# Chunk rows requested two steps sooner, and two heads' scores joined in one tile of two banks, in a gated cross-attention and feed-forward kernel

## What is computed

```python
def _layernorm(x, eps=1e-5): return (x - mean(x)) / sqrt(var(x) + eps)
def reference(x, ctx, mask, g_xattn, g_ffn, ...):      # x: 2 x 2048 x 512, ctx: 2 x 128 x 512
    # cross attention, 16 heads of 32, keys and values from ctx (128 rows of each batch)
    xn = layer_norm(_layernorm(x), g_x, b_x);  kvn = layer_norm(ctx, g_kv, b_kv)
    q = xn @ w_q;  k, v = split(kvn @ w_kv)
    attn = softmax(where(mask == 0, -1e9, q k^T * 32**-0.5));  out = attn v
    x = x + tanh(g_xattn) * (out @ w_proj + b_proj)
    # feed-forward, 512 -> 2048 -> 512, weights dequantised from integers and scales
    h = layer_norm(_layernorm(x), ln_gamma, ln_beta)
    z = silu(h @ w1 + fc1_bias) @ w2 + fc2_bias
    return x + tanh(g_ffn) * (x' + 0.5 * z)            # x' is the layer-normed input of the block
```

## Time and profile before

| | us |
|---|---|
| median of 3 runs (lowest, highest) | 1244.69 (1244.65, 1246.11) |
| profiled execution, its own time | 1246.29 |
| span of the profiled execution | 1244.7 |
| PE busy in the span | 1112.7 (89%) |
| DVE, ACT, POOL busy | 631.7, 388.1, 338.4 |
| attention stage, to the first feed-forward product | about 0 to 515 |

### The profile page before, as it was taken

One profiled execution on the slowest core, in us unless ns is written; L12 is line 12 of the kernel. 1 busy time (PEld: TensorE's weight loads), 2 busy tenths in 40 slices (PEclk: granted clock), 3 DMA queues, 4 the chain that ended last, 5 costly groups with the idle time before them and its releaser, 6 DMA issues.

```text
span 1244.7 us, 15876 instructions
## 1 busy us (share of the span) xinstructions
PE 1112.7 (89%) x5433; PEld 851.2 (68%) x5433; DVE 631.7 (51%) x1039; ACT 388.1 (31%) x614; POOL 338.4 (27%) x344
## 2 busy tenths in 40 slices
PE   5668779796978895899999999999999999999998
PEld 3345456464645563688888888888888888888887
DVE  6755757576675763777533533433434335235222
ACT  3347445464645573234111112111112111111110
POOL 4433546454554653401210210210111012012000
PEclk9779899898989898999999999999999999999999
DMA  6434353534444344790100100100100100100000
GB/s 241 94 92 107 84 141 88 139 96 117 113 124 132 82 120 140 253 316 10 36 33 1 64 5 1 68 1 1 67 0 0 67 0 0 68 1 1 34 1 34
DMA packets 56570, 92.44 MB, mean 74 GB/s; under 512 B 12952, under 2 KB 14144, under 8 KB 56000
## 3 DMA queue, kind: packets, MB, share of 16 engines
q1 hardware_dynamic: 55752, 91.54, 25.0%
q10 hardware_dynamic: 760, 0.14, 0.1%
HBM read 47.34 MB, written 16.78 MB: 52 GB/s over the span
## 4 chain that ended last, share of the span: by engine, by line
PE 58%; DVE 0%; issue 0%; ACT 0%; DVEq 0%
PE ps_y L220 10%; PE ps_y L219 10%; PE ps_y L218 9%; PE ps_z L1209 9%; PE ps_z L1211 9%; PE ps_z L1210 9%; PE ps_h L1223 1%; DVE x L1292 0%; DVE w_lo L176 0%; DVE w_f L170 0%; ACT w_hi L161 0%; DVE y_hi L1269 0%; ACT y_f L1244 0%; DVEq L47 0%; DVE y_lo L1271 0%
## 5 line engine op out<-in xcount | busy, mean ns | idle before, releaser
L1269 DVE CAST y_hi<-y_f 128x512 fp32r<-128x512 f32 x128 | 62.6, 489 | 390.7 <-ACT y_f L1244 390.7
L1244 ACT ACTIVATE y_f<-ps_y,cols 128x512 f32<-128x512 f32 x128 | 88.1, 689 | 551.7 <-PE ps_y L220 551.7
L218 PE MATMUL ps_y<-xt_hi,w_hi 128*128 128x512 f32 x512 | 202.5, 396 | 1.9 <-PEq L255 1.9
L220 PE MATMUL ps_y<-xt_hi,w_lo 128*128 128x512 f32 x512 | 204.1, 399 | 0.0
L1209 PE MATMUL ps_z<-w_hi,y_hi 128*128 128x512 f32 x512 | 202.6, 396 | 1.4 <-DVE w_lo L176 1.4
L219 PE MATMUL ps_y<-xt_lo,w_hi 128*128 128x512 f32 x512 | 203.5, 397 | 0.0
L1211 PE MATMUL ps_z<-w_hi,y_lo 128*128 128x512 f32 x512 | 200.1, 391 | 0.0
L1210 PE MATMUL ps_z<-w_lo,y_hi 128*128 128x512 f32 x512 | 199.9, 390 | 0.0
L218 PEld LDWEIGHTS ps_y<-xt_hi,w_hi 128*128 128x128 f32 x512 | 96.6, 189 | 25.2 <-issue 2.3
L219 PEld LDWEIGHTS ps_y<-xt_lo,w_hi 128*128 128x128 f32 x512 | 96.9, 189 | 22.9
L220 PEld LDWEIGHTS ps_y<-xt_hi,w_lo 128*128 128x128 f32 x512 | 96.5, 189 | 22.6
(11 more groups left out here) (161 smaller groups left out, 1593.1 us busy)
## 6 DMA issues: line engine op xcount, KB each, us to landing
q_pack<-q_hi SPq DMA_DIRECT2D x256, 64.0 KB, 2.0
x_in<-in_x SPq DMA_DIRECT2D x8, 1024.0 KB, 5.9
q_pack<-q_lo SPq DMA_DIRECT2D x128, 64.0 KB, 2.0
x_res<-in_x SPq DMA_DIRECT2D x32, 256.0 KB, 3.2
x_dram<-x_out SPq DMA_DIRECT2D x32, 256.0 KB, 3.3
q_raw<-in_L_ffn_fc_q SPq DMA_DIRECT2D x8, 1024.0 KB, 15.2
s_raw<-in_L_ffn_fc_scales SPq DMA_DIRECT2D x8, 1024.0 KB, 16.7
x_in<-x_dram SPq DMA_DIRECT2D x4, 1024.0 KB, 5.4
```

The costliest lines, as they stand in the source:

```text
L218: nc.tensor.matmul(out, s_hi, m_hi, start=(k == 0), stop=False)
L220: last = nc.tensor.matmul(out, s_lo, m_hi, start=False, stop=(k == n - 1))
L1244: nc.scalar.activation(y_f[f % 2][:, :], ps_y[f % 2][:, :], ACT.Silu, bias=b1_c[:, f:f + 1]).then_inc(y_f_ready, 1)
```

## The change

Two edits. First, `load_x` moves: chunk 0 is loaded at step -8 as before, and chunk c (1 to 8) at the head of SP's step 4c - 10 instead of 4c - 8. SP's steps are all written out now, none is in a hardware loop. Second, heads go in pairs: `ps_s` is one tensor of two banks, the scores of heads 0 and 1 fill it, then one `p_f` and one `p_hi` activation of 128x1024 empty it, and then heads 2 and 3 use it. DVE subtracts pair 0 in one instruction and POOL pair 1 in one. On PE the scores of heads 2 and 3 now stand behind both halves of the projection.

```diff
+        p_f = [sb(f"p_f{n}", [P, 2, CHUNK], F32) for n in range(2)]     (p_hi, p_lo alike)
-        ps_s = [psum("ps_s0"), psum("ps_s1")]
+        ps_s = scope.enter_context(nc.psum_tensor("ps_s", [P, 2, 512], F32))
...
-                if k % KB == 0:
-                    load_x(i, k // KB + 2)
+                if k == FIRST:
+                    load_x(i, 0)
+                if k % KB == 2:
+                    load_x(i, k // KB + 3)
...
-            every_step(sp, step, {-8: load_context, -7: load_weights, -3: pack_keys})
+            setup = {-8: load_context, -7: load_weights, -3: pack_keys}
+            for k in range(FIRST, LAST):
+                if k in setup:
+                    setup[k]()
+                step(0, k)
...
-                after(pe, p_hi_ready, HG * v + j - 1)
-                nc.tensor.matmul(ps_s[j % 2][:, :], k_pack[...], q_pack[...],
+                after(pe, p_hi_ready, 2 * v + j // 2)
+                nc.tensor.matmul(ps_s[:, j % 2, :], k_pack[...], q_pack[...],
                                  start=True, stop=True).then_inc(s_done, 1)
...
                 if real(i, k - 5, UNITS):
                     project(i, k - 5, first)
+                if real(i, k - 5, UNITS):
+                    project(i, k - 5, second)
                 if real(i, k, UNITS):
                     scores(i, k, 2)
                     scores(i, k, 3)
-                if real(i, k - 5, UNITS):
-                    project(i, k - 5, second)
...
-            def probabilities(i, k, j):
+            def probabilities(i, k, pair):
-                after(act, s_done, HG * v + j + 1)
-                after(act, p_lo_dve if j < HG // 2 else p_lo_pool, HG // 2 * (v - 1) + j % (HG // 2) + 1)
-                nc.scalar.activation(p_f[j][:, :], ps_s[j % 2][:, :], ACT.Exp, bias=fill_col[:, b:b + 1]).then_inc(p_f_ready, 1)
+                after(act, s_done, HG * v + 2 * pair + 2)
+                after(act, (p_lo_dve, p_lo_pool)[pair], v)
+                nc.scalar.activation(p_f[pair][:, :, :], ps_s[:, :, :], ACT.Exp, bias=fill_col[:, b:b + 1]).then_inc(p_f_ready, 1)
                 after(act, pv_done, v)
-                nc.scalar.activation(p_hi[j][:, :], ps_s[j % 2][:, :], ACT.Exp, bias=fill_col[:, b:b + 1]).then_inc(p_hi_ready, 1)
+                nc.scalar.activation(p_hi[pair][:, :, :], ps_s[:, :, :], ACT.Exp, bias=fill_col[:, b:b + 1]).then_inc(p_hi_ready, 1)
...
-                nc.vector.tensor_tensor(p_lo[j][:, :], p_f[j][:, :], p_hi[j][:, :], ALU.subtract).then_inc(p_lo_dve, 1)
+                nc.vector.tensor_tensor(p_lo[0][:, :, :], p_f[0][:, :, :], p_hi[0][:, :, :], ALU.subtract).then_inc(p_lo_dve, 1)
...
-                nc.gpsimd.tensor_tensor(p_lo[j][:, :], p_f[j][:, :], p_hi[j][:, :], ALU.subtract).then_inc(p_lo_pool, 1)
+                nc.gpsimd.tensor_tensor(p_lo[1][:, :, :], p_f[1][:, :, :], p_hi[1][:, :, :], ALU.subtract).then_inc(p_lo_pool, 1)
```

More of the change, by code:

```diff
@@ L287, in attention @@
             k_top, k_rest = (tmp(n, [P, KB, B * KEYS], F32R) for n in ("k_top", "k_rest"))
-        p_f = [sb(f"p_f{n}", [P, CHUNK], F32) for n in range(HG)]
-        p_hi = [sb(f"p_hi{n}", [P, CHUNK], F16) for n in range(HG)]
-        p_lo = [sb(f"p_lo{n}", [P, CHUNK], F16) for n in range(HG)]
+        p_f = [sb(f"p_f{n}", [P, 2, CHUNK], F32) for n in range(2)]
+        p_hi = [sb(f"p_hi{n}", [P, 2, CHUNK], F16) for n in range(2)]
+        p_lo = [sb(f"p_lo{n}", [P, 2, CHUNK], F16) for n in range(2)]
         inv_den, den_t = sb("inv_den", [P, CHUNK], F32), sb("den_t", [P, CHUNK // HEAD, HEAD], F32)
@@ L311, in attention @@
         ps_ctx, ps_cols = ps_max, ps_o
-        ps_k, ps_v = [ps_s[0], ps_s[1], ps_den, ps_max[0]], [ps_o, ps_den]
+        ps_k, ps_v = [ps_s[:, 0, :], ps_s[:, 1, :], ps_den, ps_max[0]], [ps_o, ps_den]
         (vec_loaded, ctx_loaded, mask_loaded, gate_loaded, wk_loaded, wv_loaded, wq_loaded, wp_loaded, bias_loaded, ident_ready,
@@ L514, in scores @@
                     after(pe, max_packed[k % 2], 16 * HG * (before_in_slot(i, k) + 1))
-                after(pe, p_hi_ready, HG * v + j - 1)
-                nc.tensor.matmul(ps_s[j % 2][:, :], k_pack[0:PACK, j, m, b * KEYS:(b + 1) * KEYS], q_pack[k % 2][0:PACK, j, :],
+                after(pe, p_hi_ready, 2 * v + j // 2)
+                nc.tensor.matmul(ps_s[:, j % 2, :], k_pack[0:PACK, j, m, b * KEYS:(b + 1) * KEYS], q_pack[k % 2][0:PACK, j, :],
                                  start=True, stop=True).then_inc(s_done, 1)
@@ L522, in weighted_values @@
                 v, b, m = PER * i + k, (k // KB) % 2, k % KB
-                after(pe, p_hi_ready, HG * (v + 1))
-                after(pe, p_lo_dve, HG // 2 * (v + 1))
-                after(pe, p_lo_pool, HG // 2 * (v + 1))
+                after(pe, p_hi_ready, 2 * (v + 1))
+                after(pe, p_lo_dve, v + 1)
+                after(pe, p_lo_pool, v + 1)
                 after(pe, o_f_ready, v)
@@ L530, in weighted_values @@
                         h = HG * m + j
-                        nc.tensor.matmul(ps_o[HEAD * j:HEAD * (j + 1), :], part[:, b, h * HEAD:(h + 1) * HEAD], probs[j][:, :],
+                        nc.tensor.matmul(ps_o[HEAD * j:HEAD * (j + 1), :], part[:, b, h * HEAD:(h + 1) * HEAD], probs[j // 2][:, j % 2, :],
                                          start=(n == 0), stop=(n == len(terms) - 1))
@@ L534, in weighted_values @@
                     for j in range(HG):
-                        last = nc.tensor.matmul(ps_den[HEAD * j:HEAD * (j + 1), :], ones16[:, :], probs[j][:, :],
+                        last = nc.tensor.matmul(ps_den[HEAD * j:HEAD * (j + 1), :], ones16[:, :], probs[j // 2][:, j % 2, :],
                                                 start=(n == 0), stop=(n == 1))
@@ L714, in step @@
                 if real(i, k, UNITS):
-                    for j in range(HG):
-                        probabilities(i, k, j)
+                    probabilities(i, k, 0)
+                    probabilities(i, k, 1)
                 if real(i, k - 1, UNITS):
@@ L810, in normalise, with probabilities_lo @@
                 nc.vector.tensor_tensor(o_f[k % 2][:, :], ps_o[:, :], inv_den[:, :], ALU.mult).then_inc(o_f_ready, 1)
[L812 removed]
+            def probabilities_lo(i, k):
                 v = PER * i + k
[L814 removed]
+                if isinstance(i, int) and v == 0:
                     dve.wait_ge(setup_over, 2)
[L816 to L818 removed]
+                after(dve, p_f_ready, 2 * v + 1)
+                after(dve, p_hi_ready, 2 * v + 1)
+                nc.vector.tensor_tensor(p_lo[0][:, :, :], p_f[0][:, :, :], p_hi[0][:, :, :], ALU.subtract).then_inc(p_lo_dve, 1)
             def add_residual(i, k):
@@ L983, in x_lo, with probabilities_lo @@
                                         ALU.subtract).then_inc(xt_lo_ready, 1)
-            def probabilities_lo(i, k, j):
+            def probabilities_lo(i, k):
                 v = PER * i + k
-                if isinstance(i, int) and v == 0 and j == 2:
+                if isinstance(i, int) and v == 0:
                     pool.wait_ge(setup_over, 2)
-                after(pool, p_f_ready, HG * v + j + 1)
-                after(pool, p_hi_ready, HG * v + j + 1)
-                nc.gpsimd.tensor_tensor(p_lo[j][:, :], p_f[j][:, :], p_hi[j][:, :], ALU.subtract).then_inc(p_lo_pool, 1)
+                after(pool, p_f_ready, 2 * v + 2)
+                after(pool, p_hi_ready, 2 * v + 2)
+                nc.gpsimd.tensor_tensor(p_lo[1][:, :, :], p_f[1][:, :, :], p_hi[1][:, :, :], ALU.subtract).then_inc(p_lo_pool, 1)
             def row_scales(i, c):
```

12 lines of the change are left out of this document (5 added, 7 removed).

## The result

The changed kernel takes 1191.87 us (median of 3 runs, 1190.06 to 1192.41) against 1244.69: a ratio of 0.957, 95% interval 0.955 to 0.959. The profiled execution has a span of 1190.5 us and a mean granted clock of 0.974. 1191.8 was predicted.

What follows compares the result with a forecast made beforehand. Load stalls bound attention before, SP's DMA issuing after. Terms -55.8 + 2.9 = -52.9 us take the profiled execution from 1246.3 to 1193.4, carried to the median as 1191.8 us; 8-of-10 range 1173 to 1208.

Steps and rivals of the forecast that it cites:

- The stalls: Seven chunk loads: the 8 us idle of DVE and PE goes, no PE wait for maxima over 1 us.
- The pairs: Ordinary attention step: two activations 2.2 us, pair 1 scores at 3.35, step 10.7 us, 0.5 less than now.
- SP after both: Attention runs at SP's pace, 11.69 us a step; 29 steps sum to 340.6 us, unit 31's maxima 55.8 us sooner.
- PE's wait in each step: In attention PE waits about 1 us for the copied maxima before the first pair of scores in each step.
- The end: Last attention unit: weighted values at 11.1 us after its scores, 2.9 us more with nothing to hide it.
- Rival A: Attention: SP is not the bound, chunks take the compute side's 44.3 us against SP's 47.4; 1173 us; chance 0.10.
- B: Attention: SP's step is 12.1 us, 12 us lost, 1204; up to 1220 with PE's clock lower; chance 0.16.
- C: Chunk load still late behind SP's own queue; only the pairs act, 0.5 us in 25 steps, 1232; chance 0.02.
- Rival D: Attention: waits in each step bring PE to 1.2 GHz, slower than before; fully low 1410 us; chance 0.02.
- a sign against itself: PE's clock falling in ordinary attention steps would show the prediction wrong; no size was given.

Runs made afterwards that it cites:

- Experiment 1: The kernel before with the earlier chunk load and SP's steps written out, but heads' scores apart as before: 1187.33 us, ratio 0.952.
- experiment 5: The changed kernel with the residual load and the store of a tile issued by ACT instead of SP: 1166.09 us, ratio 0.936.
- 6: The kernel before with early load and SP written out, heads apart, plus residual load and store issued by ACT instead of SP: 1181.45 us.
- experiment 3: The changed kernel with one more DMA of 512 bytes issued by SP in each of the steps 2 to 30: 1208.47 us.
- experiment 9: The changed kernel with the chunk's load behind the four copies of the maxima and ahead of the query copies in SP's step: 1191.20 us.
- Experiment 7: The changed kernel; in step 31 second-pair scores stand between the projection's halves, and SP issues weight loads behind the copied maxima: 1184.00 us.
- experiment 11: The changed kernel with residual load and store on ACT, step 31's second-pair scores between projection halves, weight loads behind copied maxima: 1168.09 us.

## Why the prediction was right, and where it was not

*The stalls.* Right: the wait for `x_in` is gone but for 0.3 us, PE's longest wait for maxima is 1.2 (1 was said). Experiment 1 shows that this edit alone makes the gain.

*The pairs.* In the steady steps every term held: two activations with starts 1.01 us apart end after 2.1 (2.2 predicted), pair 1 at 3.27 (3.35), ACT idle 1.07 (1.1), PE's wait 0.23 (0.25), step 10.6 (10.7). That the gain has no use while SP is slower is shown by 1 against the changed kernel, and by 5 against 6.

*SP after both.* The step that carries the prediction, and right: 29 steps took 338.7 us where the sum had 340.6, experiment 3 moves the time by an issue's whole price, and experiment 5 gives back 25.8 us, 22.3 of them in the 29 steps, in which SP has 52 issues less. The term was too long by 1.9 us, and its start by 1.3 (79.26 against 80.6: I had taken off PE's first stall of 6.6 us, and SP came 8.0 sooner). Its picture of 11.69 as SP's step hides two parts: an undisturbed 11.2 (243.42 to the next at 254.62), and stretched groups. Of the 116 groups of four copies between the maxima of unit 2 and those of unit 31, 16 took over 2.6 us in place of 2.45, 9.7 us more in sum, 0.3 a step. It was so before the change too (16 groups, 10.1 us) and with SP's steps written out in the kernel before (15 groups, 8.8 us), so written-out code is not the cause.

*PE's wait in each step.* Wrong in form. I expected 1 us before each first pair of scores. PE instead runs several steps of 10.6 to 11.5 us and then waits at once, where the copies stand behind the chunk's load: 0.3, 3.2, 3.3, 2.4 and 0.7 us in five chunks. The mean is SP's all the same, and experiment 9 shows that the place of the load does not matter.

*The end.* The term that was mis-sized: 2.9 us predicted, 5.0 measured. The weighted values came 11.5 us after the scores (11.1 reckoned), and 1.6 us more were lost behind them, between the weighted values and the feed-forward (21.5 against 19.9), which the sum had at nothing. I had also taken the 6.5 us of PE's wait before unit 31 as given. Experiment 7 shows that it came from the weight loads ahead of four small copies. The 3.2 us of SP's start and steps and the 2.1 of this one have opposite signs. The profiled executions, on which the prediction counts, fell by 54.2 us of span against 52.9 predicted, the medians by 52.8. So the 0.1 us between prediction and result is luck: the parts were right to 2 or 3 us, and the three runs alone lie 2.4 us apart.

*Rival A and the rule that issuing is small.* The Trainium skill (DMA: Bandwidth & Descriptors, Issuing engines are not separate DMA queues) says that spreading DMAs over engines saves only the time that initiating them takes, usually small beside the DMA itself. For a single copy the trace agrees: 0.6 us of SP's time, 2.0 from issue to landing. For the kernel it was 26 us of 1192 (experiment 5), since the sum of the issues was the longest chain.

*Rivals B and C.* Not met: SP's mean step was 11.68 and not 12.1, with stretched groups in both kernels alike, and the load is issued 18.8 us ahead of its use.

*Rival D, the clock.* Not met as a cost, but the clock did fall in two of the steady steps, and the prediction had named a clock that falls in ordinary steps as a sign against itself. Two waits of the changed kernel, and windows (start and end, length, busy time of the engines, granted clock, DMA share, GB/s) around them, around the wait at 238 and around the end:

```profile
189.25 1.19 PE L522 MATMUL ps_s<-q_pack,k_pack 97*128 97x512 f32 x2 [3.16 <-issue]
189.00:192.40 3.40, 3.15 (x8) 2.50 (x9) 0.00 (x0) 1.92 (x2) 0.15 (x1) 0.50 0.45 110
235.00:260.00 25.00, 21.25 (x137) 14.96 (x138) 17.89 (x34) 14.40 (x18) 15.68 (x16) 1.00 0.50 135
284.40 1.02 PE L522 MATMUL ps_s<-q_pack,k_pack 97*128 97x512 f32 x2 [2.40 <-issue]
284.60:288.00 3.40, 3.40 (x9) 2.65 (x9) 0.32 (x1) 2.12 (x2) 0.00 (x0) 0.50 0.41 98
415.00:462.00 47.00, 28.68 (x134) 19.48 (x135) 16.13 (x21) 9.77 (x12) 16.80 (x11) 0.75 0.53 170
```

The granted clock stays at full (2.4 GHz) over the wait of 3.28 us at 238.24, but behind the waits of 3.16 and 2.40 us it is at half (1.2 GHz) in the stretches shown, and the projection's matmuls take 0.63 in place of 0.40 there. So the length of one wait does not tell whether the clock falls. With SP as the bound the mean step stayed SP's all the same. In the last window, the end, the clock is at half from 417.8 to 434.7 and from 438.3 to 445, with waits of 4.7, 6.5 and 4.7 us (before 418.76, 428.46 and 439.97). The Trainium skill (TensorE: Matmul & The Clock Gate, HAM oscillation — how this bites in real kernels) describes a loop that waits for a DMA in every turn and starts each turn cold. The step of the earlier trace rows agrees with one turn of it (half clock behind a wait of 8.04 us). No run here has such a wait in every step, so the loop itself was not put to the test.

## What to carry to other kernels

Count the DMAs that each engine issues in a step and multiply by the time of one issue: an engine without a busy row can be the bound, and one issue moved to an idle engine, or one added, shows it. When a stall is taken out, ask which engine used it, and what is late next; a gain on the compute side (here the pairs) is then worth nothing until that engine is relieved, and may cost something at the end of the stage, where nothing hides it. The best kernel here (experiment 5, 1166.1 us) differs from the changed one by two issues a step. As long as the issuing engine is the bound, small copies that something waits for go ahead of large loads in the last step too (7.9 us in experiment 7); with that engine relieved it gave nothing (experiment 11).

## What was not expected of the hardware

The same DMA takes less of ACT's time than of SP's: the store 0.35 to 0.37 us on ACT (experiment 5) and mostly 0.43 to 0.46 on SP in the written-out steps, the residual load 0.34 to 0.82 on ACT (0.47 in the mean) and 0.53 to 0.59 on SP. In the steps of SP's loop in the kernel before both take mostly 0.33 to 0.44. Groups of four copies on SP, 2.45 us as a rule, take up to 3.7 in about one of seven cases, in loops as in written-out code. What stretches them was not tried. Four copies behind two weight loads take 3.9 us to issue and their reader starts 10.5 us after their issue begins; ahead of the loads it is 2.4 and 4.2.
